# Holding each eighth indirect DMA for the front, the gates and the experts; gates kept in PSUM, state scans moved, expert sums made on TensorE

## What is computed

```python
# 1. tokens: 3x3 unfold, a sigmoid gate on each of 9 taps x 64 channels
h1 = relu(t @ W1 + b1);  s = sigmoid(h1 @ W2 + b2);  h = (t * s) @ W3 + b3
# a class token is put ahead of the 3136 tokens of each image (50192 nodes in all)
# 2. a diagonal two-state linear recurrence along each image's tokens, with LayerNorm ahead
h = h + ssm(layernorm(h))
# 3. mixture of 4 experts, gated by graph attention; x = layernorm(h)
hg = (x @ W_gat).reshape(M, 4, 4)                  # 4 heads x 4 experts
e = leaky_relu(a_src[src] + a_dst[dst])            # 262144 random edges among 16384 nodes, and self loops
agg = segment_softmax_sum(e, hg[src], dst)         # over the edges that end at a node
scores = layernorm(agg + b_gat).mean(heads);  g = softmax over the top 2 of 4
out = h + sum_e g[e] * (gelu(x @ W1[e] + b1[e]) @ W2[e] + b2[e])
```

## Time and the profile before

| | us |
|---|---|
| median of 3 runs | 5600.37 |
| lowest, highest | 5581.59, 5612.91 |
| profiled execution, its own time | 5620.4 |
| its span (first to last instruction) | 5618.7 |

### The profile page before, as it was taken

The page is one execution under the profiler, slowest core; times in us unless marked ns, Lnnn a source line. Parts: engine busy times, 40 slices in busy tenths (PEclk is TensorE's granted clock), DMA queues, the critical chain, the costliest instruction groups (busy, mean ns, idle before and its releaser), DMA issues.

```text
span 5618.7 us, 27673 instructions
## 1 busy us (share of the span) xinstructions
PE 1949.2 (35%) x7311; PEld 805.7 (14%) x7311; DVE 2297.3 (41%) x3986; ACT 1167.0 (21%) x1699; POOL 2415.2 (43%) x2473
## 2 busy tenths in 40 slices
PE   0611258591148173626442225151524344000000
PEld 0211113230013031212111102020202111000000
DVE  9899438480148172535435504040403010211237
ACT  0300025250024041313221203030313233000000
POOL 0000530547721707162535472726253553677571
PEclk9855579795569596857675657575757676555555
DMA  3100124241114132222213212121212122111023
GB/s 77 36 0 0 29 45 80 42 87 17 18 33 92 23 65 48 54 38 51 56 19 49 42 27 55 16 56 15 57 19 60 38 64 64 47 23 32 18 56 116
DMA packets 651776, 247.81 MB, mean 44 GB/s; under 512 B 552244, under 2 KB 632420, under 8 KB 649188
## 3 DMA queue, kind: packets, MB, share of 16 engines
q1 hardware_dynamic: 573700, 216.76, 16.6%
q0 software_dynamic: 77920, 29.29, 5.3%
HBM read 152.68 MB, written 91.71 MB: 43 GB/s over the span
## 4 chain that ended last, share of the span: by engine, by line
another core or an unknown queue 31%; PE 20%; DVE 14%; issue 14%; POOL 7%; DVEq 6%; ACT 3%; DMA 2%; SPq 1%; ACTq 0%; POOLq 0%
POOL ring L746 7%; DVE res L1233 3%; DVEq L1235 3%; PE ps L842 3%; PE ps L832 3%; PE ps L857 2%; PE ps L946 2%; DMA arena<-xnT 2%; DVE res L1566 1%; PE ps L968 1%; PE ps L957 1%; PE ps L883 1%; PE ps L891 1%; DVE msg L1554 1%
## 5 line engine op out<-in xcount | busy, mean ns | idle before, releaser
L746 POOL DMA_INDIRECT ring<-table,src_i x2048 | 2006.2, 980 | 2030.3 <-DVEq L1570 1379.6
L1578 DVE TENSOR_TENSOR arena<-arena 128x448 f32<-128x448 f32 x504 | 295.2, 620 | 596.8 <-issue 297.9
L842 PE MATMUL ps<-arena,w 64*128 64x448 f32 x896 | 265.6, 674 | 545.7 <-ACT arena L1048 300.7
L946 PE MATMUL ps<-arena 64*128 64x512 f32 x800 | 252.7, 748 | 518.5 <-DMA arena<-xnT 242.5
L1048 ACT ACTIVATE arena<-ps,tb 128x448 f32<-128x448 f32 x504 | 298.3, 631 | 620.2 <-remote 325.4
L1727 DVE TENSOR_TENSOR arena<-ps,arena 128x1024 f32<-128x1024 f32 x68 | 83.3, 1225 | 808.3 <-remote 609.0
L712 POOL DMA_INDIRECT ring<-keys_d,place x128 | 125.9, 984 | 630.3 <-DVEq L1190 589.8
L968 PE MATMUL ps<-ident,arena 128*128 128x128 f32 x800 | 140.7, 327 | 625.7 <-issue 414.3
L857 PE MATMUL ps<-arena,w 128*64 128x448 f32 x896 | 210.1, 592 | 350.8 <-issue 350.8
L1128 ACT ACTIVATE arena<-ps,arena 128x1024 f32<-128x1024 f32 x200 | 215.1, 1115 | 401.5 <-remote 266.8
L723 POOL DMA_INDIRECT adst_d<-res,place x128 | 137.6, 1075 | 352.6 <-DVEq L1515 215.7
(11 more groups left out here) (331 smaller groups left out, 3502.2 us busy)
## 6 DMA issues: line engine op xcount, KB each, us to landing
arena<-in_x SPq DMA_DIRECT2D x304, 110.0 KB
ring<-table,src_i POOLq DMA_INDIRECT x2048
partial<-res SPq DMA_DIRECT2D x16, 1536.0 KB
arena<-in_x SPq DMA_DIRECT2D x160, 140.0 KB
outputs_d<-arena SPq DMA_DIRECT2D x32, 512.0 KB
arena<-outputs_d SPq DMA_DIRECT2D x32, 512.0 KB
arena<-xnT SPq DMA_DIRECT2D x100, 128.0 KB
arena<-h_tok SPq DMA_DIRECT2D x50, 256.0 KB
```

What stands on the lines that cost most here:

```text
L746: g.indirect_dma_start(out=ring[k % 2][:, j - k * SC, :], out_offset=None, in_=table[0:GRAPH_NODES, :], in_offset=off(ap=src_i[:, j:j + 1] ...
L842: mm(bank(1 + (2 * i + z) % 3)[:, 0:CHUNK], w2[lower_upper(z), i * P:(i + 1) * P], h1[lower_upper(z), :], start=True, stop=True).then_inc( ...
L946: m = mm(hid[ee % 2][:, z * NT:(z + 1) * NT], fw1[lower_upper(z), ee, :], xf[q][lower_upper(z), :], start=True, stop=True)
L1578: v.tensor_tensor(r3(prod[:, t, :]), tap_view(s, t), r3(gate[t % 3]), ALU.mult)\
```

## The change

**Holding.** Each eighth indirect DMA of POOL gets one more wait. In the front it is for `prod_done`, at a rate of so many DMAs per step: 14 for the key blocks from step 4, 15 for the scatters from step 14, 23 for the gathers from step 22, with a lead of 24 DMAs. Gather 816 and five later ones wait for signals of the three gate batches, and from gather 984 on it is `yT_done`, the expert halves, at 12 gathers for each pair. What of the 2048 gathers is left after pair 50 (n above 1584) is not held.

**Chunks and scans.** The last chunk of 128 is cut into 96 and 32, so there are 17. Scans stand after steps 31, 37, 43, 49, 54 and 59, and after pairs 0, 8, 20, 31 and 41. SP fetches the scatters' rows ahead of the pixels.

**PSUM gates.** From step 23 on ACT writes the sigmoid back into the PSUM bank, and PE waits for the product (`prod_done`) instead of for the sigmoid (`gate_done`) to write a bank again.

**Moved scans.** From step 23 on all four state scans stand behind the wait for `std1_done` and ahead of `u`; their rate is read from PSUM.

**Tail.** Five node batches. DVE only multiplies by the gates; PE sums the four experts and the residual with five matmuls against the identity, ACT copies the sum out. The gate function is shortened: mean, scale and the head sums in fewer and smaller instructions.

```diff
+SIZES = [SC] * (COLS // SC - 1) + [96, 32]
-NODE_BATCHES = [(0, 40), (40, 80), (80, 112), (112, 128)]
+NODE_BATCHES = [(0, 24), (24, 56), (56, 88), (88, 112), (112, 128)]
...
+PSUM_FROM = GRAPH_STEPS + 4
-SCAN_AFTER_STEP = {31: 0, 38: 1, 44: 2, 50: 3, 56: 4}
-SCAN_AFTER_PAIR = {1: 5, 9: 6, 17: 7, 25: 8, 33: 9, 41: 10}
+SCAN_AFTER_STEP = {31: 0, 37: 1, 43: 2, 49: 3, 54: 4, 59: 5}
+SCAN_AFTER_PAIR = {0: 6, 8: 7, 20: 8, 31: 9, 41: 10}
...
+GATE = 8
+BLOCK_RATE, SCATTER_RATE, FRONT_RATE, PAIR_RATE = 14, 15, 23, 12
+LEAD = 24
+GATHER_STEP = 22
+GATHERED_AT = {816: ("g_e", 1), 832: ("gt_ready", 1), 872: ("g_e", 2), 888: ("gt_ready", 2), 920: ("g_e", 3),
+               936: ("gt_ready", 3)}
+PAIRS_FROM = 984
...
+            def front_reaches(step, n, rate):
+
+                if n > 0 and n % GATE == 0 and TILES * step + TILES * n // rate <= TILES * NSTEP:
+                    pool.wait_ge(S["prod_done"], TILES * step + TILES * n // rate)
...
+            def experts_reach(n):
+
+                if n % GATE == 0 and 0 < n - PAIRS_FROM <= PAIR_RATE * PAIRS:
+                    pool.wait_ge(S["yT_done"], 2 * (n - PAIRS_FROM) // PAIR_RATE)
...
+                    front_reaches(GATHER_STEP, j - LEAD, FRONT_RATE)
+                    gates_reach(j)
+                    experts_reach(j)
...
-                wait(pe, S["gate_done"], TILES * s + 2 * i - 1)
+                wait(pe, S["prod_done"] if s >= PSUM_FROM else S["gate_done"], TILES * s + 2 * i - 1)
...
+                for ee in range(EXPERTS):
+                    mm(o, ident[:, :], yb[hidx % 3][:, :, ee, :], start=ee == 0, stop=False)
+                mm(o, ident[:, :], hr[k % 2][:, z, :, :], start=False, stop=True).then_inc(S["halves_summed"], 1)
...
-                    wait(act, S["prod_done"], TILES * s + t - 2)
-                    a(gate[t % 3], bank(1 + t % 3)[:, 0:CHUNK], ACT.Sigmoid, bias=tb2[:, t // 2:t // 2 + 1])\
+                    if s < PSUM_FROM:
+                        wait(act, S["prod_done"], TILES * s + t - 2)
+                    a(gate_of(s, t), bank(1 + t % 3)[:, 0:CHUNK], ACT.Sigmoid, bias=tb2[:, t // 2:t // 2 + 1])\
```

227 lines of the change are left out of this document (145 added, 82 removed).

## The result

| | before | after |
|---|---|---|
| median of 6 runs each, us | 5602.14 | 5186.28 |
| lowest, highest | 5576.69, 5612.91 | 5162.78, 5220.89 |
| profiled execution, its own time | 5620.4 | 5194.46 |

The ratio is 0.927, 95% interval 0.923 to 0.932: faster by 416 us, where 965 had been forecast. The time lies in the range, above the middle.

What follows compares the result with a forecast made beforehand. It took dense trains of gathers on POOL, which nearly stop all other engines, as the bound. Terms -75 - 33 - 390 - 511 + 78 - 37 = -968 from 5620.4 gave 4652 us profiled, median 4635 us; range 4150 to 5580.

Steps and rivals of the forecast that it cites:

- Holding: POOL's indirect DMAs in front and pairs: holds cut the dense trains; 36 us per step and 20.5 us per pair.
- 34 steps of 36: Front steps 22 to 55: 1224 us, with five scans at 24 us 1344 instead of 1734.4, so -390 us.
- The pairs: Expert pairs: 50 at 20.5 us plus five scans at 9 us, 1070 us instead of 1581.1, so -511 us.
- What the other edits cost: Front: moved scans' 3.2 us of PE waiting per step covered by POOL's pace; PSUM gates and SP's order zero.
- The signs that I had named for being right: Front steps of 33 to 39 us, no ACT or PE idle over some 20 us, pairs of 18 to 23 us.
- The scatters: Front, scatters to step 21: half of the 67 us lost in one step comes back, -33 us.
- Last steps and gates: Last front steps and gate batches: 178 gathers, 222 us, and as many scans as before; change 0 from 221.3 us.
- The tail: End of kernel: shorter last scan -15 us, new node batches with PE summing -22 us, together -37 us.
- Rival 1: Dense law: short trains fare like long ones, 39.8 us per step, 27.4 per pair; 5185 us; chance 0.20.
- Nothing hides: Front and pairs: each gather costs 1.25 us and each step 21.2 wherever they stand; 5578 us; chance 0.10.
- rival 5: POOL's holds do not hold: counts always reached, trains only longer; ends as Rival 1 does; no chance of its own.
- Rival 4: Slower: each held group of eight pays a recovery; 6019 us at 8 us each, 7230 at 15; chance 0.08.

Runs made afterwards that it cites:

- standing sets: Sets of runs in which the kernel before took 5526 to 5569 us, as in the case itself; dense gather trains stop the other engines.
- free sets: Sets of runs in which the kernel before took 4072 to 4080 us; nothing stands still beside the gathers.
- the kernel with both undone: Changed kernel with its holds, but gates in SBUF and state scans in their old places: 4821.2 us beside 5569.4 for the kernel before, ratio 0.862.
- the second standing set: The changed kernel as it is, run again beside the kernel before: 5131.8 us beside 5560.2, ratio 0.924.

## Why the prediction was right and wrong

**What bounds the kernel: right in these runs, but a condition, not a property.** The dense train stops the others in standing sets, and I had taken it for the nature of gathers. In free sets the same kernel runs 27% shorter, and POOL's pace is the bound.

**Holding: right, and nearly of the size that I forecast.** Of the 551 us by which the time misses (5186 against 4635), some 310 are the two moves, by the kernel with both undone. With nothing moved the front takes 1404 us; my sum had 1344. The term "34 steps of 36" comes out as (1404 - 120) / 34 = 37.8 us. The pairs: my 20.5 us plus 9 for a scan. From pair 2 on after takes 4248.3 - 3247.9 = 1000 us for 48 pairs with four scans, or 20.1 us each. What my sum lacked there are the first two pairs: 184 us with 130 gathers, against 50 in my sum for two pairs and a scan. Only 886 gathers had been issued by then, and as the hold goes from gather 984 on, what was missing came as a dense train. These 134 us, less 20 that the other 48 pairs came out better, are the 115 by which the pairs miss.

**What the other edits cost: wrong, and this is the step that failed.** I wrote that "a step of 36 us is not bound by PE", so that POOL's pace would cover the moved scans, and put PSUM gates at zero. The size of the uncovered wait, 3.2 us, was right: 3.0 were measured. But nothing covers it. In a standing set a step is a sum: the front's own time, plus POOL's time beyond the 12 to 15 us that hide. Whoever lengthens the front's own time pays in full. Without the standstill the two moves lengthen it by 6.0 us (3.0 of PE waiting for `u`, 1.1 for products, 1.9 in PE's own instructions at the lower mean clock), and half of this comes with the PSUM gates alone. In the standing set they cost 7.5; where the other 1.5 arise was not traced. That is 254 us of the 322 by which the front misses; of the rest, 60 are 37.8 against 36, and 8 lie between the two standing sets. The signs that I had named for being right failed here too: the three steps shown took 48 us and not 33 to 39, and ACT stood 21.5 us in a step. I thought of two rows side by side, of which the longer counts; they stand one behind the other.

**The scatters: wrong.** Half of the 67 us lost in one step was to come back. A step of 71 us with 36 scatters is still there: they wait for stored rows and then come in a row. That the counts had been reached by then is argued, not tried.

**Key blocks, gathers after the pairs: right** (-83 for -75, +88 for +78).

**Last steps and gates: +35, of which 24 by like cuts,** where 0 had been put; the waits for gate signals were given no price. With both moves undone this stretch took 207.1 us, with them 280.5 in the second standing set: what stands there is how far the gathers are behind when the front ends. That link was not tried by itself.

**The tail: -37 forecast, 0 measured, but not for want of the gain.** From the first node gather to the last, and from there to the end, before and then after:

```profile
5340.20:5521.70 181.50, 0.00 (x0) 0.00 (x0) 70.72 (x129) 2.74 (x8) 128.84 (x128) 0.50 0.24 57
5521.70:5618.70 97.00, 0.00 (x0) 0.00 (x0) 80.63 (x160) 2.36 (x8) 1.29 (x1) 0.50 0.45 143
```

```profile
4912.50:5112.80 200.30, 51.16 (x163) 40.08 (x164) 66.66 (x127) 9.54 (x28) 128.78 (x127) 0.60 0.27 72
5112.80:5192.50 79.70, 40.44 (x159) 33.22 (x157) 39.16 (x85) 8.18 (x24) 0.94 (x1) 0.78 0.37 124
```

Behind the last node gather the new tail is 17.3 us shorter, near the 22 that I took, and the sign that I had named for being wrong (not under 90 us) did not come. But the node gathers take 18.8 us more: POOL waits twice for DVE to have used a batch, 18.7 and 13.6 us, where it waited once, 12.6 us. I had not priced the wait that a fifth batch adds. And the stretch before them, with the last scan, gave 1.6 us (43.8 to 42.2) instead of 15. In free sets the tail is 275.8 to 251.9, -24: the stretch with the scan gives 14.1 us there (39.5 to 25.4), POOL does not wait for the batches of the new tail at all, and the end gives 7.2. The kernel without holds and moves has 195 and 80 us for these two stretches in its standing set, so the wait needs neither holds nor moves. That it is the standstill which makes DVE late there is argued from the free sets, not tried.

**The rivals.** Rival 1, the dense law, gave 5185 us, and 5186 were measured. That is chance: it had pairs of 27.4 us (they took 20 to 21) and front steps of 39.8 (by the same reckoning they took (1665.8 - 120) / 34 = 45.5). Its rule, that short trains fare like long ones, falls in the pairs. "Nothing hides" comes near the front (50 us per step) only because the moves lengthen it; in place it was 37.8. Of rival 5 half is true: the counts of three groups are reached together, and 24 go out as one train. Rival 4, a recovery for each held group, is refuted: a hold in each step, with 12 gathers, left the step at 21.2 us. The 15.0 us for which I had seen DVE held after a train were 4 to 5 us here for PE and ACT.

**The rule of the Trainium skill** that I weighed, "SBUF — State Buffer", "Who interferes with whom": DMA never contends with a compute engine, and TensorE and ScalarE wait on no one. Free sets agree (21.2 us per step with 15 gathers), and so do plain DMAs in a standing one (50.9 against 48.5). The 557.7 us of L1165 in the standing run do not, and the measurement decides.

## What to carry to other kernels

Before adding a wait that spreads a disturbing work, measure how much of that work hides beside one step; here it was 14 to 15 us of gathers beside a step, and what is beyond is paid wherever it stands. So the aim is that no step goes without its share, and that a pause comes before more than some ten follow each other: trains of 12 with a pause were free beside a step, trains of 8 beside a pair, and longer ones were not. Look in the trace whether the holds do part them. Where two works add up instead of overlapping, an edit that lengthens the other one is paid in full: this change would have given 0.862 instead of 0.924 without its two moves. And let the kernel before run in more than one set: the holds that are worth 723 us in one kind of set (nothing moved) cost 61 us in the other (both moved), where GpSimd only needed to be left alone.
